# A three-stage vision block on one core: free steps by doubling, constants in two parts, TensorE's mixture work in another order

## The reference

```python
# tokens: each 4x4 patch becomes one token, 256 tokens of 64 channels an image
reduce = x_patches.mean(pixels)                       # (64, 256, 64)
q  = layernorm(reduce, ln_q) @ Wq.T
kv = layernorm(pixels_of_patch, ln_kv) @ Wkv.T        # 16 pixels a patch
h  = reduce + softmax_over_pixels(q*k, 8 heads) . v @ proj_w.T + proj_b
# state-space part, 256 time steps, A diagonal (a), dt = 1/256, s = 1/(1+dt*dt*a)
x_new = s*x - dt*s*a*z + dt*s*Bu
z_new = dt*s*x + s*z + dt*dt*s*Bu
y = gelu(z @ W_C.T + b_C + h @ W_D.T + b_D);  out = y*sigmoid(y) + h
h = layernorm(h + out)
# mixture: shared MLP 64-64-128-64, four experts 64-128-64-64, top 2 by softmax gates
h = layernorm(h + shared(h) + sum_top2(weight * expert(h)))
```

## Time and profile before

| what | us |
|---|---|
| median of 3 runs (lowest, highest) | 1020.04 (1019.95, 1021.08) |
| the profiled execution: its own time | 1021.32 |
| its span, first to last instruction | 1019.5 |
| PE busy | 943.5 (93%) |
| DVE busy | 761.7 (75%) |
| ACT busy | 501.4 (49%) |
| POOL busy | 436.1 (43%) |
| mean granted TensorE clock | 0.977 of full |

### The profile page before, as it was taken

How to read it: one execution, slowest core, us unless ns; L and a number is a source line. 1 busy time by engine, 2 the same in 40 slices (tenths; PEclk the granted TensorE clock), 3 DMA queues, 4 the chain that set the end, 5 groups by cost and what they waited for, 6 DMA issues and landing times.

```text
span 1019.5 us, 24614 instructions
## 1 busy us (share of the span) xinstructions
PE 943.5 (93%) x9608; PEld 368.8 (36%) x9608; DVE 761.7 (75%) x1290; ACT 501.4 (49%) x799; POOL 436.1 (43%) x259
## 2 busy tenths in 40 slices
PE   4569999999999999999999989996999999999996
PEld 1114344343434334343434443232333333333332
DVE  6678787878778787878878776998566766766664
ACT  3335454554545454454545412265465664655753
POOL 3237676777767677776767720000110100101000
PEclk9769999999999999999999999998899999999999
DMA  9128878787887878787887742000000000000000
GB/s 384 33 65 234 263 212 264 212 247 230 240 257 218 262 214 247 228 241 251 225 256 217 215 110 58 0 1 0 0 12 21 10 10 21 10 16 15 10 22 22
DMA packets 64007, 141.47 MB, mean 139 GB/s; under 512 B 22576, under 2 KB 22576, under 8 KB 55728
## 3 DMA queue, kind: packets, MB, share of 16 engines
q1 hardware_dynamic: 63920, 140.18, 47.1%
HBM read 68.85 MB, written 4.19 MB: 72 GB/s over the span
## 4 chain that ended last, share of the span: by engine, by line
PE 82%; DVE 11%; issue 3%; DMA 1%; POOL 1%; ACT 1%; SPq 0%; DVEq 0%; POOLq 0%
PE ring L798 20%; PE bank_ms L770 11%; PE qp L835 11%; PE bank_sq L770 5%; PE ring L991 5%; DVE sb_prodv L1152 4%; PE ring L1002 4%; PE bank_ms L1032 3%; PE qp L969 2%; PE bank_sq L991 2%; PE ring L985 2%; PE ring L932 2%; PE bank_ms L1002 2%; PE bank_ms L1024 2%; PE bank_sq L1011 1%
## 5 line engine op out<-in xcount | busy, mean ns | idle before, releaser
L798 PE MATMUL ring<-sb_arena,sb_wqkv 64*64 64x512 f32 x2048 | 269.4, 609 | 37.8 <-DVE sb_prodk L1121 20.2
L1152 DVE TENSOR_TENSOR sb_prodv<-ring,sb_wbc 128x1024 f32<-128x1024 f32 x128 | 154.1, 1207 | 32.6 <-PE ring L798 30.2
L1121 DVE TENSOR_TENSOR sb_prodk<-ring,sb_qbuf 128x1024 f32<-128x1024 f32 x128 | 153.4, 1220 | 20.6 <-PE ring L798 18.1
L405 POOL TENSOR_TENSOR sb_rows<-sb_arena 128x2048 f32<-128x2048 f32 x31 | 141.4, 4562 | 14.8 <-DMA sb_arena<-x 14.8
L534 POOL TENSOR_TENSOR sb_parts_q<-sb_arena,sb_const 128x512 fp32r<-128x512 f32 x15 | 15.6, 1040 | 305.6 <-ACT sb_arena L654 305.6
L835 PEld LDWEIGHTS qp<-sb_prodv,sb_tok_w 64*64 64x64 f32 x4096 | 119.6, 133 | 54.7 <-issue 51.4
L835 PE MATMUL qp<-sb_prodv,sb_tok_w 64*64 64x128 f32 x4096 | 128.4, 269 | 2.5 <-DVE sb_prodv L1152 2.5
L577 ACT ACTIVATE sb_xsq<-sb_arena 128x2048 f32<-128x2048 f32 x64 | 118.5, 1899 | 6.9 <-DMA sb_arena<-x 6.9
L798 PEld LDWEIGHTS ring<-sb_arena,sb_wqkv 64*64 64x64 f32 x2048 | 59.1, 133 | 172.9 <-issue 83.4
L501 POOL TENSOR_TENSOR sb_score<-sb_score,sb_smx 128x512 f32<-128x512 f32 x32 | 41.0, 1281 | 105.1 <-DVE sb_smx L1135 105.1
L407 POOL TENSOR_TENSOR sb_rows<-sb_rows 128x1024 f32<-128x1024 f32 x31 | 73.9, 2384 | 2.4
(11 more groups left out here) (198 smaller groups left out, 1489.1 us busy)
## 6 DMA issues: line engine op xcount, KB each, us to landing
sb_arena<-x SPq DMA_DIRECT2D x64, 1024.0 KB, 8.7
sb_wbc<-sb_wgt SPq DMA_DIRECT2D x256, 256.0 KB, 5.7
out<-sb_arena SPq DMA_DIRECT2D x64, 64.0 KB, 1.9
sb_rest_w<-rest_w SPq DMA_DIRECT2D x1, 918.5 KB, 22.1
sb_const<-const SPq DMA_DIRECT2D x1, 520.5 KB, 8.1
sb_tok_w<-tok_w SPq DMA_DIRECT2D x1, 260.5 KB, 2.8
```

Of the source, the lines that this page charges most:

```text
L405: eng.tensor_tensor(rows[:, :, :, :], pix[:, :, 0:8], pix[:, :, 8:16], ALU.add).then_inc(sum8_ready, 1)
L798: mm = pe.matmul(ring[slot][C * half:C * half + C, i, :], image_block(w, i), x[C * i:C * i + C, m, half, c], start=True, stop=True)
L1121: dve.tensor_tensor(by_pixel(prodk[:, c]), by_pixel(ring[c % 2][:, :, :]), q[:, :, None, :].to_broadcast([P, 2, N_PIX, G32]), ALU.mult).th ...
L1152: dve.tensor_tensor(prodv[:, :, :, G32 * c:G32 * (c + 1)], by_pixel(ring[k % 2][:, :, :]), by_pixel(wbc[:, c]), ALU.mult).then_inc(values_ ...
```

## The change

1. **Free steps by doubling.** One step is computed as before. From k known steps the next k follow at once: `double_steps(k)` for k = 1, 2, 4, 8, each two `tensor_scalar` on 128 x 2k elements and then two `scalar_tensor_tensor`, with one wait after each two. All of it stands ahead of the patch sums of pair 0, and the pieces in the lead-in are gone.
2. **Constants in two parts.** The first 529 columns come ahead of the first `x`, the last 512 (used in the mixture alone) after the last load of the start, with a semaphore of their own.
3. **The mixture's order on PE.** `centre_rows` is one iteration ahead, not two, and stands behind the first shared layer; `out_rows` comes ahead of the experts; the second shared layer stands directly behind the first layers of the experts (k = 9, 10, the second layers are now k = 11 to 14); `turn_routing` behind all second layers; the bias matmuls ahead of the third layers. ACT's and DVE's orders follow.

```diff
-N_COEFS = 14 + 3 * L
+N_COEFS = 17 + 4 * 4
-        cacc = sb("cacc", P, 2)
+        cacc = sb("cacc", P, 2, L // 2, 2)
-        K_SHARED, K_SPREAD, K_SUM, USES = 13, 15, 19, 20
+        K_SHARED, K_SECOND, K_SPREAD, K_SUM, USES = 9, 11, 15, 19, 20
...
             sp.dma_start(tok_w[:, :], t["tok_w"]).then_inc(tok_in, 16)
+            sp.dma_start(const[:, 0:K_SEL], t["const"][:, 0:K_SEL]).then_inc(const_in, 16)
             load(0)
-            sp.dma_start(const[:, :], t["const"]).then_inc(const_in, 16)
             for u in range(1, NF):
                 load(u)
             sp.dma_start(rest_w[:, :], t["rest_w"]).then_inc(rest_in, 16)
+            sp.dma_start(const[:, K_SEL:K_END], t["const"][:, K_SEL:K_END]).then_inc(select_in, 16)
...ACT, one iteration
                     norm_sq(i + 1)
-                relu(act, i, 1)
                 act.wait_ge(logits_shifted, i + 1)
                 act.activation(lgx, lgx, ACT.Exp).then_inc(logits_exp, 1)
-                for k in (3, 4, 5, 6):
+                if prev:
+                    out_sq(i - 1)
+                for k in (1, 3, 4):
                     relu(act, i, k)
                 act.wait_ge(gates_shifted, i + 1)
                 act.activation(pick, pick, ACT.Exp).then_inc(gates_exp, 1)
-                relu(act, i, 8)
-                if prev:
-                    out_sq(i - 1)
-                relu(act, i, 9)
+                for k in (5, 6, 8, 9, 10):
+                    relu(act, i, k)
                 if nxt:
                     norm_rstd(i + 1)
-                relu(act, i, 10)
                 if prev:
                     out_rstd(i - 1)
-                relu(act, i, 11)
+                for k in (11, 13, 14):
+                    relu(act, i, k)
                 act.wait_ge(routing_turned, i + 1)
                 act.activation(in_order(route[0:2 * E, :]), by_group(bank_var[0:2 * E, :]), ACT.Copy).then_inc(routing_high, 1)
-                relu(act, i, 13)
-                relu(act, i, 14)
...PE, one iteration
                 pe.matmul(ring_use(i, 0)[:, :], sw1, h2[:, p, :], start=True, stop=True).then_inc(ring_mm, 1)
+                if nxt:
+                    centre_rows(i + 1)
                 turn_logits(i)
+                if prev:
+                    out_rows(i - 1)
                 for e in range(E):
...
-                    if e == 0 and prev:
-                        out_rows(i - 1)
+                pe.wait_ge(taken[0], USES // RING * i + 1)
+                pair = [ring_use(i, K_SHARED + m) for m in range(2)]
+                for m in range(2):
+                    rows = slice(C * m, C * m + C)
+                    pe.matmul(pair[m][:, :], sw2[rows, :], h1s[rows, :], start=True, stop=True).then_inc(ring_mm, 1)
                 if nxt:
                     variance(i + 1)
...
                     mm.then_inc(ring_mm, 1)
-                    if k == 11:
-                        turn_routing(i, nxt)
-                pe.wait_ge(taken[0], USES // RING * i + 1)
-                pair = [ring_use(i, K_SHARED + m) for m in range(2)]
-                for m in range(2):
-                    rows = slice(C * m, C * m + C)
-                    pe.matmul(pair[m][:, :], sw2[rows, :], h1s[rows, :], start=True, stop=True).then_inc(ring_mm, 1)
-                if not isinstance(i, int) or i + 2 < ITERS:
-                    centre_rows(i + 2)
+                turn_routing(i, nxt)
                 pe.wait_ge(routing_low, i + 1)
...
+                pe.matmul(bank[:, :], exact[0:N_ROUTE, H_B3:H_SEL], route[0:N_ROUTE, :], start=True, stop=False,
+                          skip_group_check=True)
+                pe.matmul(bank[:, :], b3_low[0:N_ROUTE, :], route[0:N_ROUTE, :], start=False, stop=False,
+                          skip_group_check=True)
...the third layers follow, start=False
-                for w in (exact[0:N_ROUTE, H_B3:H_SEL], b3_low[0:N_ROUTE, :]):
-                    pe.matmul(bank[:, :], w, route[0:N_ROUTE, :], start=False, stop=False, skip_group_check=True)
...DVE, lead-in
+            def double_steps(k):
+                n_coefs[0] += 2
+                for a, acc in ((cz, 0), (cv, 1)):
+                    dve.tensor_scalar(cacc[:, acc, 0:k, :], cv[:, 1:k + 1, :], a[:, k, 1:2], None, ALU.mult).then_inc(coefs, 1)
+                dve.wait_ge(coefs, n_coefs[0])
+                n_coefs[0] += 2
+                for a, acc in ((cz, 0), (cv, 1)):
+                    dve.scalar_tensor_tensor(a[:, k + 1:2 * k + 1, :], cz[:, 1:k + 1, :], a[:, k, 0:1], cacc[:, acc, 0:k, :],
+                                             ALU.mult, ALU.add).then_inc(coefs, 1)
+                dve.wait_ge(coefs, n_coefs[0])
+            for k in (1, 2, 4, 8):
+                double_steps(k)
...
-            free_steps(0, 4)
-            free_steps(4, 13)
-            free_steps(13, L)
...DVE, one iteration
+                relu(dve, i, 12)
                 if not isinstance(i, int) or i + 1 < ITERS:
                     normed(i + 1, (p + 1) % 2)
-                relu(dve, i, 12)
-                route_low(i)
                 if prev:
                     finish(i - 1, (p + 1) % 2)
+                route_low(i)
```

More of the change, by code:

```diff
@@ L198, in build @@
         tok_in = sem("tok_in")
+        select_in = sem("select_in")
         rest_in = sem("rest_in")
@@ L929, in centre_rows @@
                 pe.wait_ge(normed_ready, i)
-                if isinstance(i, int) and i == 3:
+                if isinstance(i, int) and i == 2:
                     pe.wait_ge(residual_ready, 2 * N_RES)
@@ L1023, in mstep @@
                 for im in range(2):
-                    pe.matmul(bank[C * im:C * im + C, :], sw3[:, :], h2s[:, im], start=True, stop=False,
+                    pe.matmul(bank[C * im:C * im + C, :], sw3[:, :], h2s[:, im], start=False, stop=False,
                               skip_group_check=True)
-                for w in (exact[0:N_ROUTE, H_B3:H_SEL], b3_low[0:N_ROUTE, :]):
-                    pe.matmul(bank[:, :], w, route[0:N_ROUTE, :], start=False, stop=False, skip_group_check=True)
                 for q in range(2):
@@ L1044, in _ @@
             logits(0, 0)
-            centre_rows(1)
             mixture(pe, mstep)
@@ L1071, in _ @@
             link(dve.scalar_tensor_tensor(svc(SV_NM), svc(SV_A), -1.0, svc(SV_S), ALU.mult, ALU.mult))
+            for a, n in ((cz, 0), (cz, 1), (cv, 0), (cv, 1)):
+                link(dve.memset(a[:, 0, n:n + 1], float((a is cz) == (n == 0))))
+            link(dve.tensor_scalar(cacc[:, 0, 0, :], cz[:, 0, :], svc(SV_NM), None, ALU.mult))
+            link(dve.scalar_tensor_tensor(cv[:, 1, :], cv[:, 0, :], svc(SV_S), cacc[:, 0, 0, :], ALU.mult, ALU.add))
+            link(dve.tensor_tensor(cz[:, 1, :], cz[:, 0, :], cv[:, 1, :], ALU.add))
+            def double_steps(k):
[10 more added lines that the diff above has]
+                double_steps(k)
             link(dve.tensor_scalar(svc(SV_F), svc(SV_S), DT * DT, None, ALU.mult))
@@ L1077, in _ @@
             link(dve.tensor_tensor(svc(SV_G), svc(SV_G), svc(SV_NM), ALU.add))
-            for a, n in ((cz, 0), (cz, 1), (cv, 0), (cv, 1)):
-                link(dve.memset(a[:, 0, n:n + 1], float((a is cz) == (n == 0))))
-            def free_steps(first, last):
-                for j in range(first, last):
-                    link(dve.tensor_scalar(cacc[:, :], cz[:, j, :], svc(SV_NM), None, ALU.mult))
-                    link(dve.scalar_tensor_tensor(cv[:, j + 1, :], cv[:, j, :], svc(SV_S), cacc[:, :], ALU.mult, ALU.add))
-                    link(dve.tensor_tensor(cz[:, j + 1, :], cz[:, j, :], cv[:, j + 1, :], ALU.add))
-            free_steps(0, 4)
+            assert n_coefs[0] == N_COEFS
             patch_sums(dve, 0, 0)
@@ L1390, in weigh @@
                 q, m = n // 2, n % 2
-                kr = 9 + n
+                kr = K_SECOND + n
                 dve.wait_ge(taken[kr % RING], USES // RING * i + kr // RING + 1)
```

16 lines of the change are left out of this document (8 added, 8 removed).

## The result

| | us |
|---|---|
| kernel before, median of 4 runs (lowest, highest) | 1020.6 (1020.0, 1021.9) |
| changed kernel, median of 4 runs (lowest, highest) | 1037.9 (1034.5, 1038.5) |
| ratio, 95% interval | 1.0161 (1.0136 to 1.0186) |
| profiled execution of the changed kernel: own time, span | 1038.1, 1036.3 |

The forecast was 1010.8, with 999 to 1020 as range. The time lies outside it on the slow side, and none of the rivals names the cause.

What follows compares the result with a forecast made beforehand. The prediction took PE to bound most of the span and DVE's row the lead-in. Lead-in -22.0 and mixture +12.8 (16 iterations of +0.8) sum to -9.2 us: 1010.8 us as a median, range 999 to 1020.

Steps and rivals of the forecast that it cites:

- the three steps: Lead-in, DVE's last three free steps: without them `pixel_var(1)` follows at once, -10.6 us.
- The clock: Lead-in, from `pixel_var` to the score: PE's clock no longer falls, -5.5 us (bounds 0 and -6.2).
- rival B: The clock falls in the lead-in all the same, as PE pauses at every key product: 1016.3 us; chance 0.12.
- The nine steps: Lead-in: `pixel_var(0)` moves from 29.61 to 21.8, -7.8 us; the work ahead of the patch sums costs +1.1.
- no gain by itself: Lead-in: early transfer of the constants' first half gains nothing; `x`, 0.65 us later, still lands before the patch sums.
- The +0.8 for POOL: Lead-in: POOL's patch sums of pair 2 come 1 us after ACT needs them, +0.8 us.
- Rival D: Lead-in gain not kept: weight spread or POOL holds pair 0's values, only -10 there, 1022.8 us; chance 0.04.
- -1.4 for the shapes: Mixture, PE: fewer changes of tile shape save 1.4 us per iteration.
- +1.55 for the wait: Mixture: PE waits between `turn_routing` and the spread for ACT and DVE, +1.55 us per iteration.
- +0.65 for the ring: Mixture: the fifth pair in a row waits for banks that ACT must read, +0.65 us per iteration (0 to 1.0).
- rival A: The mixture breaks even: ACT keeps ahead and the order does what its name says, 998 us; chance 0.16.
- C: Slower: ACT's reads become the bound of the mixture, +1.6 us an iteration, 1023.6 us; chance 0.08.

Runs made afterwards that it cites:

- e9: Kernel before with only the constants in two parts; 1022.6 us, ratio 1.0014.
- e3_fill: Changed kernel plus one needless full matmul per iteration in the wait behind `turn_routing`; 1009.3 us, ratio 0.9883.
- e1_lead_only: Kernel before with the doubling and the constants in two parts, mixture in its old order; 1000.1 us, ratio 0.9801.
- e11: e8 with ACT's `out_rstd` behind its copy of the routing weights and DVE's `finish` behind `route_low`; 984.8 us, ratio 0.9640.
- e8: e7 with ACT's `out_sq` and exponential of the gates moved behind reads 5 and 6; 991.5 us, ratio 0.9716.
- e6: Changed kernel with `turn_routing` one second layer earlier (behind k = 13), ACT's copy ahead of read 14; 997.1 us, ratio 0.9767.
- e7: Changed kernel with `turn_routing` two second layers earlier (behind k = 12), ACT's copy ahead of reads 13 and 14; 993.8 us, ratio 0.9735.
- e4: Kernel before with `turn_routing` moved directly ahead of the spread, ACT's copy behind its last two reads, nothing grouped; 1073.9 us, ratio 1.0517.
- e5: Changed kernel plus the same needless matmul per iteration, behind the variance sums where PE has no wait; 1050.9 us, ratio 1.0298.
- e2: Kernel before with only the mixture's new order, old lead-in kept; 1058.4 us, ratio 1.0364.

## Why the prediction was wrong

**Right: the lead-in.** Forecast -22.0, measured -22.1 at the score of pair 1 and -22.7 at the mixture's start. Its terms, from the rows: the three steps, forecast -10.6; from the score of pair 0 to `pixel_var(1)` it is 37.95 - 31.87 = 6.08, against 57.04 - 40.22 = 16.82, so -10.7. The clock, forecast -5.5; from `pixel_var` to the score 7.78 and 7.55 against 10.61 and 10.55, so -5.8, and the clock held at 1.00, as rival B said it would not. The nine steps with what stands ahead of them, forecast -6.7; `pixel_var(0)` 24.09 against 29.61, -5.5.

The miss of 1.2 has two parts. The first is the part called "no gain by itself": the split was counted to delay nothing, `x` at 0.65 us later. It landed about 2.1 later (11.07 against 8.93; 1.0 in e9), and DVE, ready at 10.44, waited 0.69; the patch sums start at 11.13 and not at 10.5. The second is PE's clock in its first work, for which there was no term. The same 16 matmuls (the pixel sums) in the changed kernel and in e3_fill, whose lead-in is the same:

```profile
18.43 3.64 PE L770 MATMUL bank_ms<-sb_arena,sb_const 128*32 128x512 f32 x16
```

```profile
18.38 2.59 PE L770 MATMUL bank_ms<-sb_arena,sb_const 128*32 128x512 f32 x16
```

At the full clock such 16 take 1.89. In the changed kernel the full level is on record from 22.3 us on, in e3_fill from 19.8, and there `pixel_var(0)` stands at 22.84, although its patch sums start at 11.09. So about 1 us of this term differs from one execution to the next.

Part of the fit is luck, too. In e3_fill the clock falls in the lead-in all the same, from 40.3 to 47.1 us, and the score of pair 1 comes at 46.48; in e1_lead_only it comes at 44.22. Rival B happened there in part; it did in one of the ten profiled executions with the doubling. And one reading in the forecast was wrong without harm: the clock before was not down from 26.3 to 67. It was full again from 40.0 to 50.2, between two falls, and both stretches from `pixel_var` to the score lie in these falls but for 0.2 and 0.3 us.

The +0.8 for POOL did not come. Rival D (the gain is not kept) is out.

**Right: the mixture but for the clock.** The terms were -1.4 for the shapes, +1.55 for the wait, +0.65 for the ring, +0.8 in all. An iteration was to take 19.3. The one in which the clock did not fall took 19.12, which is +0.63. Its wait is 1.46; the other two terms together are 0.63 - 1.46 = -0.83, against -1.4 + 0.65 = -0.75, and e11, without a wait, bears that out (17.60 - 18.49 = -0.89). How this divides between the two I had wrong. The five pairs take 5.09 in a row, and 3.06 + 2 x 1.06 = 5.18 before: a pair takes about 1.0 us in either order and not 0.86, no new wait for a ring bank is shown beyond the 0.12 of e8, and joining the pairs wins 0.1. The reader should note that 0.28 of the 3.06 was put down to the ring without a row that names it; what it is stays open. So rival A (no wait) and C (ACT the bound, 1.6 an iteration or more) are both out in their mechanism. C's size was the closest to the truth, for another reason: PE's waits are released by the routing, not by reads of ACT. By the rule of the Trainium skill named with C ("TensorEngine Tiling (Array Packing)", "Performance Considerations") the emptying of PSUM would have been the bound; the trace does not agree, with 0.12 us at most that moved with ACT's reads. L1347, the subtraction of the maximum (L1339 before), took 0.19 us: POOL's work began just behind it, and the rule on the shared port did not come into play.

**Wrong: "+1.55 (1.4 to 1.8)", the price of the wait.** The step priced a PE wait at its own length. It assumed, without a word, that the mixture keeps the clock of 1.00 of the earlier trace rows. The same text weighed the clock in the lead-in, and stopped short of asking it where PE was to get a new wait each iteration. What the runs put in its place: the wait is 1.54 us and brings on average 1.9 us more at 1.2 GHz behind it. The sum: (313.3 - 284.5) = 28.8 us over 15 distances, 284.5 being the same sum in e3_fill, which differs by one matmul in the idle time. The clock's own record says the same: half of the 58.0 us at 1.2 GHz is 29.0. With that, -22.0 + 12.8 + 28.8 is +19.6; measured are +17.3 (the median) and +16.8 (the span).

**How far the cause is shown.** That the idle stretch between `turn_routing` and the spread brings the clock down is shown from three sides: filled, the fall goes (e3), shortened by order, it goes (e6, e7), made without the grouping, it comes (e4); and the same matmul elsewhere does not help (e5). Waits of 0.36 to 0.61 us brought no fall in any iteration of e3, e6, e7 and e8. In the changed kernel, e2, e4 and e5, with 1.41 to 1.54 us in nearly all iterations, one followed in 54 of 64; of the two longest waits, 2.01 us in the last iterations of e4, one brought none. Why a given iteration is spared, or stays at 1.2 GHz twice as long, is left open, as is what a length between 0.61 and 1.41 would do: no run had one.

## What to carry to other kernels

A new wait on an engine that bounds a stage costs its length and, on TensorE, what the clock loses behind it: ask of each new recurring wait, even one of 1.5 us, whether the clock is still full, and look for it as matmuls of double length *behind* the wait. When matmuls are grouped by shape (worth 0.9 us an iteration of 18.5 here), keep enough of them between a result and its use by another engine's detour: the gain of e11 over the changed kernel, 53 us, is the same grouping with two second layers left as cover, and with the detour's instructions earlier in their engines' rows. If no useful cover is left, a needless matmul is one (e3).
